# MoE routing: router weights as a zero-padded stationary tile, softmax and top-k by halves of the batch, most tiles normalised on ScalarE

## What is computed

```python
def _layernorm(x):                      # over the 128 features
    return (x - mean(x)) / sqrt(var(x) + 1e-05)

def _L0_ffn_ref(x, router_w, w1, b1, w2, b2):       # x is the normalised activation
    capacity = int(256 * 2.0 / 8) + 1               # 65 tokens for each expert
    scores = softmax(einsum('bsd,ed->bse', x, router_w), axis=-1)     # 8 experts
    gate_vals, sel_idx = top_k(swapaxes(scores, 1, 2), capacity)      # along the 256 tokens
    tokens = x[b_idx, sel_idx]
    h = gelu(einsum('becd,edh->bech', tokens, w1) + b1)
    y = einsum('bech,ehd->becd', h, w2) + b2
    out = zeros_like(x).at[b_idx, sel_idx].add(y * gate_vals[..., None])
```

## Time and profile before

| | |
|---|---|
| median of 3 runs | 3446.3 us (3445.3 to 3448.44) |
| the profiled execution: its own time | 3451.66 us |
| its span, first to last instruction | 3449.9 us |
| busy: PE, DVE, ACT, POOL | 3035.3, 2443.9, 1752.3, 1381.5 us |
| mean granted TensorE clock, as a share of full speed | 0.912 |
| first routing: first bn_stats to end of the last cast | 452.53 to 529.47 us |
| second routing: the same | 1668.82 to 1745.78 us |

### The profile page before, as it was taken

How to read it: one execution, slowest core, us unless ns; L and a number is a source line. 1 busy time by engine, 2 the same in 40 slices (tenths; PEclk the granted TensorE clock), 3 DMA queues, 4 the chain that set the end, 5 groups by cost and what they waited for, 6 DMA issues and landing times. The chain is left out here.

```text
span 3449.9 us, 51677 instructions
## 1 busy us (share of the span) xinstructions
PE 3035.3 (88%) x17140; PEld 2018.0 (58%) x17140; DVE 2443.9 (71%) x5884; ACT 1752.3 (51%) x3844; POOL 1381.5 (40%) x1366
## 2 busy tenths in 40 slices
PE   6999966999872999998759998889799999999989
PEld 3555555888640444444648886689545555555557
DVE  5888865777564777775757775223499999999964
ACT  2545313333441899997323333235366666666644
POOL 3555411222322677777202223322144444444432
PEclk9999957999985999999679998569899999999999
DMA  3000012110132010100321100000000000000001
GB/s 115 1 1 1 1 49 77 38 54 1 29 115 76 27 30 27 30 27 20 88 77 38 48 1 27 1 1 1 1 1 1 1 1 1 1 1 1 1 13 38
DMA packets 106567, 91.43 MB, mean 27 GB/s; under 512 B 15373, under 2 KB 96147, under 8 KB 104000
## 3 DMA queue, kind: packets, MB, share of 16 engines
q1 hardware_dynamic: 104928, 87.31, 8.0%
q10 hardware_dynamic: 1376, 0.82, 0.1%
HBM read 57.66 MB, written 30.15 MB: 25 GB/s over the span
## 5 line engine op out<-in xcount | busy, mean ns | idle before, releaser
L2427 ACT ACTIVATE m_x_hT<-m_x_hid,wm_b 128x260 f32<-128x260 f32 x512 | 244.3, 477 | 422.6 <-PE m_x_hid L2366 422.6
L1318 POOL TENSOR_TENSOR c_tE<-c_tE,c_tDm 128x256 f32<-128x256 f32 x512 | 372.2, 728 | 139.6 <-ACT c_tE L1278 125.8
L1201 DVE TENSOR_REDUCE c_tM<-c_tpa 128x2 f32<-128x512 f32 x512 | 330.3, 682 | 130.9 <-PE c_tpa L1103 129.9
L1278 ACT ACTIVATE c_tE<-c_tpb 128x512 f32<-128x512 f32 x512 | 309.7, 606 | 43.4 <-PE c_tpb L1120 43.4
L2366 PE MATMUL m_x_hid<-m_x_xg,wm_w 128*128 128x260 f32 x1024 | 319.7, 396 | 1.2 <-DVE m_x_cols L2310 1.2
L2374 PE MATMUL m_x_yp<-m_x_hT,wm_w 128*128 128x260 f32 x1024 | 311.5, 388 | 0.0
L1654 POOL TENSOR_TENSOR b_wkv<-b_at,b_rec 128x512 f32<-128x512 f32 x128 | 163.1, 1275 | 306.2 <-DVE b_rec L1590 306.2
L1103 PE MATMUL c_tpa<-c_tK,c_Qm 96*128 96x256 f16 x1024 | 205.5, 284 | 49.4 <-DMA c_Qm<-aug_d 36.3
L1259 ACT ACTIVATE c_tDm<-wc_pos,c_LD 128x128 f32<-128x128 f32 x512 | 209.1, 411 | 20.5 <-PEq L96 20.5
L1120 PE MATMUL c_tpb<-c_Qm,c_tK 101*128 101x256 f16 x1024 | 198.8, 276 | 23.3 <-ACT c_tE L1278 23.3
L2374 PEld LDWEIGHTS m_x_yp<-m_x_hT,wm_w 128*128 128x128 f32 x1024 | 198.0, 193 | 31.5
(11 more groups left out here) (349 smaller groups left out, 7714.3 us busy)
## 6 DMA issues: line engine op xcount, KB each, us to landing
m_x_ir<-idx_d SPq DMA_DIRECT2D x16, 1040.0 KB, 7.3
xn_d<-xn SPq DMA_DIRECT2D x32, 256.0 KB, 2.3
m_x_xs<-xn_d SPq DMA_DIRECT2D x16, 512.0 KB, 4.1
c_tK<-k_d SPq DMA_DIRECT2D x32, 192.0 KB
c_Qm<-q_d SPq DMA_DIRECT2D x128, 48.0 KB
wm_w<-in_m_w SPq DMA_DIRECT2D x2, 2048.0 KB, 10.3
gate_d<-c_pgate SPq DMA_DIRECT2D x16, 256.0 KB
q_d<-c_phi SPq DMA_DIRECT2D x32, 128.0 KB
```

Source lines behind the costliest of these rows:

```text
L1201: nc.vector.tensor_reduce(out=M[:, u % 2, 2 * h:2 * h + 2], in_=pa[:, h % 2], axis=AX.X, op=ALU.max).then_inc(s["max_done"], 1)
L1278: nc.scalar.activation(E[:, h % 8].rearrange("p a q -> p (a q)"), pb[:, h % 2, :], ACT.Exp).then_inc(s["exp_done"], 1)
L1318: nc.gpsimd.tensor_tensor(diag, diag, Dm[:, u % 2, h:h + 1, :].to_broadcast([P, 2, P]), ALU.mult).then_inc(s["dmul_done"], 1)
L2427: nc.scalar.activation(hT[:, e % 2, j, :], hid[:, c % 2, 0:QW], ACT.Gelu, bias=w["m_b1"][:, c:c + 1]).then_inc(s["gelu_done"], 1)
```

## The change

It rewrites `stage_route` in five respects.

- The moments are made in five pieces of 1, 3, 4, 4 and 4 groups (`CUTS`), all before anything else on VectorE, and the 7 small operations run once for each piece. GpSimd makes rstd and also -mean x rstd for a piece at once, into `k.rstd_all` and `k.shift_all`.
- Groups 0 to 11 (`BY_ACT` = 12) are normalised on ScalarE, as x * rstd + shift with four `activation` operations each; groups 12 to 15 stay on VectorE. There are 4 slots of `xn` instead of 2.
- The router's 8 columns stand in the middle of a tile of zeros (`wide`). A view of 128 of its columns is now the stationary operand, and the transposed tokens of a batch, 256 columns, are the moving one. Batch b of a half writes 8 of the 128 partitions, and 16 batches accumulate into one block of rows (`lrow`); the other partitions get zeros added.
- ScalarE copies a finished block of rows to SBUF (`keep`), TensorE transposes it to tokens (`by_token`), the softmax is made for this half of the batches (`fall`, `exps`, `shares`), and TensorE transposes the scores back (`by_row`).
- The choice runs 9 rounds for block 0 and then 9 rounds for block 1. The softmax of block 1 is inserted between the rounds of block 0.

The diff, cut to its core:

```diff
+        lrow = ps("lrow", [P, 2, GW])
+        lg = ps("lg", [P, 2, GW])
+        rows = ps("rows", [P, 2, GW])
...
+        NX = 4
+        xn = sb("xn", [P, NX, GT, D])
...
+        CUTS = (0, 1, 4, 8, 12, 16)
+        PIECES = len(CUTS) - 1
...
+        HALF = NG // 2
+        BY_ACT = CUTS[-2]
...
+            def moments(p):
+                base = TICKS(p)
+                t0, n = GT * CUTS[p], GT * (CUTS[p + 1] - CUTS[p])
+                at = slice(t0, t0 + n)
+                at_least(dve, s["ln_tick"], base)
+                for i in range(n):
...
+            def fall(r):
+                dve.wait_ge(s["lg_done"], r + 1)
+                nc.vector.tensor_reduce(mx[:, r], by_expert(lg[:, r, 0:T]), AX.X, ALU.max).then_inc(s["peak"], 1)
+                dve.wait_ge(s["peak"], r + 1)
+                nc.vector.tensor_tensor(by_expert(dl[:, r]), by_expert(lg[:, r, 0:T]), spread(mx[:, r]), ALU.subtract).then_inc(s["fell"], 1)
+
+            def shares(r):
+                dve.wait_ge(s["exp_done"], r + 1)
+                nc.vector.tensor_reduce(sm[:, r], by_expert(ex[:, r]), AX.X, ALU.add).then_inc(s["total"], 1)
+                dve.wait_ge(s["total"], r + 1)
+                nc.vector.reciprocal(rs[:, r], sm[:, r]).then_inc(s["over"], 1)
+                dve.wait_ge(s["over"], r + 1)
+                nc.vector.tensor_tensor(by_expert(sc[:, r]), by_expert(ex[:, r]), spread(rs[:, r]), ALU.mult).then_inc(s["share"], 1)
+
+            def take_rows(r):
+                dve.wait_ge(s["rows"], r + 1)
+                nc.vector.tensor_copy(work[:, r], rows[:, r, 0:T]).then_inc(s["work"], 1)
+
+            def best(r, n):
+                top, eight = tops[r], slice(8 * n, 8 * n + 8)
+                if n:
+                    dve.wait_ge(top, 3 * n)
+                else:
+                    dve.wait_ge(s["work"], r + 1)
+                nc.vector.max(val[:, r, eight], work[:, r, :]).then_inc(top, 1)
+                dve.wait_ge(top, 3 * n + 1)
+                nc.vector.max_index(idx[:, r, eight], val[:, r, eight], work[:, r, :]).then_inc(top, 1)
+                if n < ROUNDS - 1:
+                    dve.wait_ge(top, 3 * n + 2)
+                    nc.vector.match_replace(work[:, r, :], val[:, r, eight], work[:, r, :], -1.0).then_inc(top, 1)
...
+            def normalise(g):
+                dve.wait_ge(s["shift_done"], PIECES)
+                at_least(dve, s["turned"], g - NX + 1)
+                dve.wait_ge(stored[g % NX], 16 * (g // NX))
                 for i in range(GT):
+                    n = g * GT + i
+                    nc.vector.tensor_scalar(xn[:, g % NX, i, :], k.X[:, n, :], k.rstd_all[:, n:n + 1], k.shift_all[:, n:n + 1],
+                                            ALU.mult, ALU.add).then_inc(s["xn_dve"], 1)
...
-            moments(0, 0)
-            for u in range(2):
...
+            for p in range(PIECES):
+                moments(p)
+            fall(0)
+            normalise(BY_ACT)
+            normalise(BY_ACT + 1)
+            shares(0)
+            normalise(BY_ACT + 2)
+            normalise(BY_ACT + 3)
+            take_rows(0)
             for n in range(ROUNDS):
-                eight = slice(8 * n, 8 * n + 8)
-                for r, top in enumerate((s["top0"], s["top1"])):
-                    if n:
-                        dve.wait_ge(top, 3 * n)
-                    nc.vector.max(val[:, r, eight], work[:, r, :]).then_inc(top, 1)
-                for r, top in enumerate((s["top0"], s["top1"])):
-                    dve.wait_ge(top, 3 * n + 1)
-                    nc.vector.max_index(idx[:, r, eight], val[:, r, eight], work[:, r, :]).then_inc(top, 1)
-                for r, top in enumerate((s["top0"], s["top1"])):
-                    if n < ROUNDS - 1:
-                        dve.wait_ge(top, 3 * n + 2)
-                        nc.vector.match_replace(work[:, r, :], val[:, r, eight], work[:, r, :], -1.0).then_inc(top, 1)
-            for r, top in enumerate((s["top0"], s["top1"])):
-                dve.wait_ge(top, 3 * ROUNDS - 1)
-                nc.vector.tensor_copy(idf[:, r, :], idx[:, r, :]).then_inc(top, 1)
+                if n == ROUNDS - 4:
+                    fall(1)
+                if n == ROUNDS - 3:
+                    shares(1)
+                if n == ROUNDS - 1:
+                    take_rows(1)
+                best(0, n)
+            indices(0)
+            for n in range(ROUNDS):
+                best(1, n)
+            indices(1)
...
+            nc.gpsimd.memset(wide[:], 0.0).then_inc(s["wide"], 1)
+            nc.gpsimd.memset(half_neg[:], -0.5).then_inc(s["rooted"], 1)
+            pool.wait_ge(s["wide"], 1)
+            nc.gpsimd.tensor_copy(wide[:, P - NE:P], w["m_router"][:]).then_inc(s["wide"], 1)
+            pool.wait_ge(s["rooted"], 1)
+            for p in range(PIECES):
+                at = slice(GT * CUTS[p], GT * CUTS[p + 1])
+                pool.wait_ge(s["ln_tick"], TICKS(p + 1))
+                nc.gpsimd.tensor_tensor(k.rstd_all[:, at], vareps[:, at], half_neg[:, at], ALU.pow).then_inc(s["rooted"], 1)
+                pool.wait_ge(s["rooted"], p + 2)
+                nc.gpsimd.tensor_tensor(k.shift_all[:, at], k.mean_neg[:, at], k.rstd_all[:, at], ALU.mult).then_inc(s["shift_done"], 1)
...
-                for i in range(GT):
-                    mm = nc.tensor.matmul(lg[:, g * GT + i, :], lhsT=xT[:, slot, i * P:(i + 1) * P], rhs=w["m_router"][:],
-                                          start=True, stop=True)
...
+            def logits(g):
                 pe.wait_ge(s["xT_ready"], g + 1)
+                if g == 0:
+                    pe.wait_ge(s["wide"], 2)
+                for i in range(2):
+                    b = 2 * g + i
+                    first = P - NE - NE * (b % RB)
+                    mm = nc.tensor.matmul(lrow[:, b // RB, 0:T], lhsT=wide[:, first:first + P], rhs=xT[:, g % 2, i * T:(i + 1) * T],
+                                          start=(b % RB == 0), stop=(b % RB == RB - 1), skip_group_check=True)
                 mm.then_inc(s["logits"], 1)
+
+            def by_token(r):
+                pe.wait_ge(s["copied"], r + 1)
                 for h in range(2):
+                    mm = nc.tensor.transpose(lg[:, r, h * P:(h + 1) * P], lr[:, r, h * P:(h + 1) * P], k.ident[:])
+                mm.then_inc(s["lg_done"], 1)
+
+            def by_row(r):
+                pe.wait_ge(s["share"], r + 1)
+                for h in range(2):
+                    mm = nc.tensor.transpose(rows[:, r, h * P:(h + 1) * P], sc[:, r, h * P:(h + 1) * P], k.ident[:])
+                mm.then_inc(s["rows"], 1)
+
+            turn_in(0)
+            turn_in(1)
+            for g in range(NG):
+                logits(g)
+                if g + 2 < NG:
+                    turn_in(g + 2)
+                if g == HALF:
+                    by_token(0)
+                if g == NG - 3:
+                    by_row(0)
+            by_token(1)
+            by_row(1)
...
         @block.scalar
         def _(act):
+            def normalise(g):
+                act.wait_ge(s["shift_done"], piece_of(g) + 1)
+                at_least(act, s["turned"], g - NX + 1)
+                at_least(act, stored[g % NX], 16 * (g // NX))
+                for i in range(GT):
+                    n = g * GT + i
+                    nc.scalar.activation(xn[:, g % NX, i, :], k.X[:, n, :], ACT.Identity, scale=k.rstd_all[:, n:n + 1],
+                                         bias=k.shift_all[:, n:n + 1]).then_inc(s["xn_act"], 1)
+
+            def evac(g):
                 act.wait_ge(s["turned"], g + 1)
+                at_least(act, s["logits"], g - 1)
+                nc.scalar.copy(xT[:, g % 2, :], turn[:, g % 2, :]).then_inc(s["xT_ready"], 1)
+
+            def keep(r):
+                act.wait_ge(s["logits"], HALF * (r + 1))
+                nc.scalar.copy(lr[:, r], lrow[:, r, 0:T]).then_inc(s["copied"], 1)
+
+            def exps(r):
+                act.wait_ge(s["fell"], r + 1)
+                nc.scalar.activation(ex[:, r], dl[:, r], ACT.Exp).then_inc(s["exp_done"], 1)
+
+            normalise(0)
+            normalise(1)
+            for g in range(NG):
+                if g + 2 < BY_ACT:
+                    normalise(g + 2)
+                evac(g)
+                if g == HALF:
+                    keep(0)
+                if g == HALF + 3:
+                    exps(0)
+            keep(1)
+            exps(1)
 
 
 def stage_experts(nc, k, tag, w, xn_d, val_d, idx_d, arrive, loads):
```

166 lines of the change are left out of this document (56 added, 110 removed).

## The result

The changed kernel takes 3423.0 us (median of 4 runs, 3422.1 to 3428.8) where the kernel before takes 3446.2 (4 runs, 3445.3 to 3448.4): a ratio of 0.9935, with a 95% interval of [0.9918, 0.9953]. 3425 was predicted, with a range of 3414 to 3438. The profiled execution is one of 3422.1 us with a span of 3420.3; that of before was 3451.7.

What follows compares the result with a forecast made beforehand. VectorE was taken to set the pace, TensorE close behind at the low clock. Savings of 9.9 plus 0.9 us a routing, 21.6 for both, took 3451.7 to 3430.1; less 5.4 for the profiled execution, 3425, range 3414 to 3438.

Steps and rivals of the forecast that it cites:

- Moments in pieces: Start of a routing: VectorE finishes all moments at 18.3 us; pieces ready for ScalarE from 3.0 to 21.8 us.
- ScalarE's period: Normalisation and copy on ScalarE: 2.04 us a group, making ScalarE the chain of the front phase.
- The clock: TensorE in the router phase: granted clock rises from 0.50 to full from about 18 us into the routing.
- the first rival: TensorE's clock stays low and it becomes the chain: a routing loses 1.3 us, 3449 us in all; 7 in 100.
- the rival that ends slower: Clock low and TensorE's period stays 2.85 instead of 2.63 us: 3.1 us more a routing, 3455; 4 in 100.
- Softmax and the early block: Softmax of block 0 by itself: block 0 copied at 37.3 us instead of 56.6, 19.3 us earlier.
- The choice: Rounds in series: 13.2 us a block, 26.4 against 19.6 for both, plus 2.8 for six inserted operations.
- Stores: End of a routing: two of four final DMAs issued during block 1's choice, saving 0.9 us.
- The sum: Both routings: 10.8 us saved in each, 21.6 together, leading to 3425 us.
- The other rivals: Slower ScalarE or GpSimd, 3434 to 3438, 15 in 100; free serial choice, 3411, 6; mishap such as table load, 4.

Runs made afterwards that it cites:

- experiment 3: Kernel before with only the wide router added, normalisation on VectorE, one softmax and paired choice kept: 3444.6 us, 0.9989 of the kernel before.
- experiment 10: Changed kernel with all 16 groups normalised on VectorE, none on ScalarE, and both blocks chosen in pairs: 3425.9 us, 0.9925 of the kernel before.
- experiment 7: Changed kernel with VectorE normalising groups 5 to 15, choice in pairs and `by_row(0)` behind the last logits: 3403.6 us, 0.9877 of the kernel before.
- experiment 6: Changed kernel with the router undone (8 columns of weights move again) and the choice in pairs: 3439.4 us, 0.9986 of the kernel before.
- experiment 1: Changed kernel with only the cut choice undone, both blocks again chosen in pairs: 3418.8 us, 0.9917 of the kernel before.
- experiment 12: Changed kernel with narrow router and paired choice, plus 100 unused identity transposes ahead of each routing's first group: 3437.8 us, one run.
- experiment 9: Changed kernel with narrow router and paired choice, every transpose of a group's tiles done twice: 3468.1 us, 1.0063 of the kernel before.
- experiment 2: Changed kernel with only the router undone, 8 columns of weights moving again: 3438.4 us, 0.9973 of the kernel before.

## Why the prediction was right, point by point

*Moments in pieces.* Right. VectorE is through with them at t = 17.5 (18.3 predicted), and the pieces reach ScalarE at the predicted times: group 0 was normalised from 456.11, t = 3.2 (3.0), group 1 from t = 7.7 (7.9). The prediction costed this part only as the supply of ScalarE. Experiments 3 and 10 show that it carries more of the gain than it was given: with a clock that rises to 1.00 in both, the last cast comes at 75.1 with moments by group and at 62.5 to 63.9 with moments in pieces, with VectorE normalising everything in both (experiment 10 has its softmax by halves and four slots besides, so the 11 to 13 us between them are not the pieces' alone; no run has the pieces by themselves).

*ScalarE's period.* Right to 0.02: 2.02 a group, block 0's maximum at 29.4 for 29.6. What the prediction did not ask is whether ScalarE was needed. Experiment 10 says hardly (at most 1.4 us a routing), and experiment 7 that the split had put VectorE's 11.92 us of idle time to no use: with seven more groups on VectorE the routing is 4 us shorter than with the same choice and twelve on ScalarE.

*The clock.* The step on which everything hung, and right: it is still low at the logits of 464.35 (2.08 us) and full at those of 469.44 (1.03), t = 16.5, where 18 was said. Experiment 6 against experiment 1 gives its price, with nothing else different but two copies and four transposes: 10.5 us a routing. And experiment 3 gives its condition: 1.7 us where VectorE sets the pace. Neither the clock alone (1.7) nor everything else alone (3.8, experiment 6) makes the gain; together they make 14.3 (76.7 to 62.5). The prediction's reason holds as far as it goes. It drew on the transposes of the earlier trace rows and the dense matmuls of the earlier trace rows, and experiment 12 confirms that transposes alone can raise the clock. But the kernel before had such transposes in every group and stood at 0.50 for 51 us, and doubling them (experiment 9) changed nothing: what kept the clock down were the 8-column matmuls between them, which the prediction noted in the stretch at 0.50 and did not name as the cause, and what the change did for the clock was to replace these. The rule of the Trainium skill against which this was weighed ("TensorE: Matmul & The Clock Gate", Part 4, that PE-mode transposes do not count as busy in the same way and the full clock does not engage for them) does not hold for the f32 transposes here: the granted clock went from 0.51 to 1.00 within the 100 transposes of experiment 12. A forecast by that rule, the first rival's 3449, would have been 26 us off.

*The first rival, a low clock.* It did not happen with the wide router; experiment 2 is the same schedule at the low clock with the narrow one. Its routing ends 9.6 us later than the changed kernel's, where the rival said 12.1, and it is 0.27% faster than the kernel before. Part of the 2.5 us between these is the narrow router itself, with a period of 2.45 and no copies or extra transposes. For the wide one at the low clock there is the one period of 2.56, below the 2.63 that was added up and just above the 2.54 at which the rival that ends slower was to begin. An estimate from these rows: 14 periods of 0.11 more and one pair of extra transposes (0.4) ahead of block 0's copy put the last cast of experiment 2 at 77.2 instead of 75.3. That is 0.5 behind the kernel before, and 0.8 to 1.2 come back in the stores. So the first rival, about as fast as before, was priced well enough, and the other one was not far off; no run has the wide router at the low clock all through.

*Softmax and the early block.* Right: block 0's copy starts at t = 37.0 for 37.3, 19.7 us earlier than that of both did.

*The choice.* Right as a cost: a block was to take 13.2 us in series and takes 13.3, a round 1.52 for 1.48 (its own durations add up to 1.50). Block 0 with the six inserted operations takes 15.2 (490.31 to 505.50), so these cost 1.9 and not 2.8: an operation of the other block fills the gap in which the next step of the round would wait. What the prediction never compared is the changed kernel with its own choice left in pairs. It set the early start of block 0 (19.3 us) against the loss in series (6.8) and called the rest a gain, as if the early start needed the cut. It does not: with the front phase as it is, both blocks are copied only 5.8 us behind block 0, and experiment 1, which gives the cut up, has its last cast 3.2 us sooner. Of the parts that were undone here, the cut is the one that costs time.

*Stores.* 0.9 was said, 1.2 measured in the first routing (4.1 us from the last cast to the next load before, 2.9 after) and 0.8 in the second (4.0 and 3.2). In experiment 1, 1.5 and about 1 come back.

*The sum.* 10.8 a routing was said; 12.3 and 11.9 were measured between the first `bn_stats` and the experts' first load, which is 1.5 and 1.1 more: 1.2 of it lie ahead of the last cast's end, most of it in the inserted operations, and the rest is the stores, 0.3 more than said and then 0.1 less. The rest of the difference between the two profiled spans, some 5 us, lies in stages that the change does not touch, and the profiled execution of before was itself 5.4 above its median, as the prediction said. What sets such differences between executions stays open; no run here was made for it.

*The other rivals.* ScalarE was not slower than its rows, no load of an activation table stands in either routing, and the choice in series was not free: in the series the instruction behind a MAX8 starts 0.46 us after it (490.35 to 490.81), in a pair the second MAX8 0.33 after the first.
